# Layer 2's experts: picking the two largest of 16 gates by two rounds of a maximum instead of comparisons in pairs

## What is computed

```python
scores = jax.nn.softmax((xf @ gate_w.T).astype(jnp.float32), axis=-1)
orig = scores
scores = scores + gate_b
sg = scores.reshape(T, 4, 4)
group_scores = jax.lax.top_k(sg, 2)[0].sum(-1)
_, gidx = jax.lax.top_k(group_scores, 2)
keep = jax.nn.one_hot(gidx, 4).sum(axis=1) > 0
scores = jnp.where(keep[:, :, None], sg, -jnp.inf).reshape(T, 16)
_, idx = jax.lax.top_k(scores, 2)
weights = jnp.take_along_axis(orig, idx, axis=1)
...
h = jax.nn.silu(h1) * h3
yo = jnp.einsum('tei,eid->ted', h, We2) + be2
y = jnp.einsum('te,ted->td', combine, yo)
```

## Time and profile before

| | us |
|---|---|
| median of 3 runs (3043.07 to 3043.55) | 3043.09 |
| the profiled execution | 3035.05 |
| its span, first to last instruction | 3033.3 |
| PE busy in the span | 2791.1 (92%) |
| DVE busy | 2149.0 (71%) |
| ACT busy | 1706.9 (56%) |
| POOL busy | 1043.7 (34%) |

### The profile page before, as it was taken

How to read it: one execution, slowest core, us unless ns; L and a number is a source line. 1 busy time by engine, 2 the same in 40 slices (tenths; PEclk the granted TensorE clock), 3 DMA queues, 4 the chain that set the end, 5 groups by cost and what they waited for, 6 DMA issues and landing times.

```text
span 3033.3 us, 68982 instructions
## 1 busy us (share of the span) xinstructions
PE 2791.1 (92%) x25484; PEld 1876.1 (62%) x25484; DVE 2149.0 (71%) x5792; ACT 1706.9 (56%) x4109; POOL 1043.7 (34%) x1420
## 2 busy tenths in 40 slices
PE   6999999989999999999998799999989988998897
PEld 2666666666666666666666455577756655556675
DVE  6888888855666566666666688665667786887674
ACT  3877777873333377777776466634335443333565
POOL 7787778731000001111112345222333321004341
PEclk9999999999999999999999899999989999999999
DMA  3110111122000011111112544100054432334660
GB/s 104 30 29 17 29 29 30 29 72 99 15 1 1 10 25 30 30 30 30 30 30 65 150 140 131 45 1 15 1 150 136 121 92 57 84 72 130 195 173 26
DMA packets 194061, 188.15 MB, mean 62 GB/s; under 512 B 14416, under 2 KB 170256, under 8 KB 192960
## 3 DMA queue, kind: packets, MB, share of 16 engines
q1 hardware_dynamic: 193728, 183.73, 23.2%
HBM read 130.36 MB, written 53.31 MB: 61 GB/s over the span
## 4 chain that ended last, share of the span: by engine, by line
PE 64%; DVE 18%; ACT 6%; issue 5%; SPq 3%; DMA 2%; POOL 2%; DVEq 0%; ACTq 0%; POOLq 0%
PE pb L160 57%; ACT big L932 4%; PE pb L629 3%; SPq L1834 2%; DVE big L2153 2%; ACT big L157 2%; DVE big L802 2%; DVE big L231 1%; DVE big L785 1%; DMA big<-parts 1%; PE pb L562 1%; DVE big L713 1%; PE pb L2124 1%; DVE big L784 1%; DVE big L176 1%
## 5 line engine op out<-in xcount | busy, mean ns | idle before, releaser
L160 PE MATMUL pb<-big 64*128 64x256 bf16 (+13 forms) x20300 | 2525.4, 331 | 157.9 <-DVE big L2153 59.1
L160 PEld LDWEIGHTS pb<-big 128*128 128x128 f32 (+5 forms) x20300 | 1576.6, 145 | 904.9 <-issue 537.5
L157 ACT ACTIVATE big<-pb 128x512 f32<-128x512 f32 (+7 forms) x1444 | 825.9, 619 | 573.9 <-PE pb L160 333.8
L157 ACT ACTIVATE big<-pb,big 128x512 f32<-128x512 f32 (+2 forms) x536 | 315.9, 616 | 607.4 <-PE pb L160 511.7
L2153 DVE TENSOR_REDUCE big<-pb 128x4 f32<-128x1024 f32 (+1 forms) x256 | 278.1, 1086 | 111.5 <-PE pb L160 108.2
L171 POOL TENSOR_TENSOR big<-big 128x128 f32<-128x128 f32 x192 | 85.0, 457 | 684.2 <-DVE big L168 684.2
L932 ACT ACTIVATE big<-big 128x256 f32<-128x256 f32 x512 | 253.9, 497 | 70.9 <-DVE big L807 69.1
L932 ACT ACTIVATE big<-pb,big 128x128 f32<-128x128 f32 (+1 forms) x512 | 255.6, 513 | 64.5 <-DVE big L787 64.2
L802 DVE CUSTOM_DVE_ANT_0 big<-pb,big 128x256 f32<-128x256 f32 x512 | 186.6, 421 | 80.2 <-PE pb L160 79.9
L1011 POOL TENSOR_TENSOR big<-big 128x512 f32<-128x512 f32 x128 | 159.8, 1276 | 243.2 <-DMA big<-recip 243.2
L1508 DVE SCALAR_TENSOR_TENSOR big<-pb,big 128x128 f32<-128x128 f32 x512 | 144.0, 344 | 139.3 <-PE pb L160 138.5
(11 more groups left out here) (138 smaller groups left out, 2290.6 us busy)
## 6 DMA issues: line engine op xcount, KB each, us to landing
big<-parts SPq DMA_DIRECT2D x96, 512.0 KB, 4.1
parts<-big SPq DMA_DIRECT2D x384, 96.0 KB, 2.3
big<-recip SPq DMA_DIRECT2D x64, 512.0 KB, 6.5
big<-comb SPq DMA_DIRECT2D x32, 512.0 KB, 8.4
parts<-big SPq DMA_DIRECT2D x192, 64.0 KB, 2.1
big<-gates SPq DMA_DIRECT2D x8, 1024.0 KB, 6.2
big<-in_wf SPq DMA_DIRECT2D x1, 3072.0 KB, 14.9
big<-scratch SPq DMA_DIRECT2D x1, 3072.0 KB, 17.6
```

The costliest lines, as they stand in the source:

```text
L157: return e.activation(o, i, f, bias=bias, scale=scale)
L160: return e.matmul(o, l, r_, start=start, stop=stop, skip_group_check=True)
```

## The change

The pieces `top_a` and `top_b` keep their places, but no longer share the tiles between them. Each now handles all four tiles, and each finds one gate of every token: `take_largest` takes the maximum of the 16 gates, marks the places that equal it, multiplies the marks by 16, 15, ... 1, takes the maximum of that (the first place that has it), marks that place, and adds -3.0e38 to the gate there. `top_a` does this once, `top_b` a second time on what is left and then adds the two marks. All elementwise instructions have 64 columns, both maxima go from 64 columns to 4.

```diff
-        TRI = alloc(336)
-        TRI16, TRI8, TRI4 = TRI[:, 0:256], TRI[:, 256:320], TRI[:, 320:336]
+        TRI = alloc(96)
+        BACK16, TRI8, TRI4 = TRI[:, 0:16], TRI[:, 16:80], TRI[:, 80:96]
...
+        def take_largest(e, own, src, picked, tmp, largest):
+            back = BACK16.unsqueeze(1).to_broadcast([128, 4, 16])
+            every = largest.unsqueeze(2).to_broadcast([128, 4, 16])
+            e.tensor_reduce(largest, src, AXX, ALU.max).then_inc(own.sem, own.up())
+            e.wait_ge(own.sem, own.n)
+            e.tensor_tensor(tmp, src, every, ALU.is_equal).then_inc(own.sem, own.up())
+            e.wait_ge(own.sem, own.n)
+            e.tensor_tensor(tmp, tmp, back, ALU.mult).then_inc(own.sem, own.up())
+            e.wait_ge(own.sem, own.n)
+            e.tensor_reduce(largest, tmp, AXX, ALU.max).then_inc(own.sem, own.up())
+            e.wait_ge(own.sem, own.n)
+            e.tensor_tensor(picked, tmp, every, ALU.is_equal).then_inc(own.sem, own.up())
+            e.wait_ge(own.sem, own.n)
+            e.scalar_tensor_tensor(out=src, in0=picked, scalar=-3.0e38, in1=src, op0=ALU.mult, op1=ALU.add).then_inc(own.sem, own.up())
...
                 elif p == "top_a":
                     e.wait_ge(own.sem, own.n)
-                    keep_top2(e, own, glv[:, 0:2, :], 2, E, TRI16, gkv[:, 0:2, :], w1, w2)
+                    take_largest(e, own, glv, gkv, v3(w1), sm[:, 80:84])
                 elif p == "top_b":
-                    keep_top2(e, own, glv[:, 2:4, :], 2, E, TRI16, gkv[:, 2:4, :], w1, w2)
+                    e.wait_ge(own.sem, own.n)
+                    take_largest(e, own, glv, v3(w2), v3(w1), sm[:, 80:84])
+                    e.tensor_tensor(gkv, gkv, v3(w2), ALU.add).then_inc(own.sem, own.up())
+                    e.wait_ge(own.sem, own.n)
                     e.tensor_tensor(cm, gpv, gkv, ALU.mult).then_inc(combined, 1)
...
-    tri = [np.tril(np.ones((E, E)), -1).reshape(-1) for E in (16, 8, 4)]
-    c["tri"] = np.broadcast_to(np.concatenate(tri), (128, 336))
+    tri = [np.tril(np.ones((E, E)), -1).reshape(-1) for E in (8, 4)]
+    c["tri"] = np.broadcast_to(np.concatenate([16 - np.arange(16)] + tri), (128, 96))
```

## The result

| | before | after |
|---|---|---|
| median, us | 3043.08 (3035.17 to 3043.55) | 3004.6 (2998.88 to 3009.76) |
| profiled execution's span, us | 3033.3 | 2996.8 |
| chunk 2 of the expert steps, us (3.4 us of it at the lower clock before) | 31.24 | 26.53 |
| an ordinary chunk that no half-speed stretch touches, us | 29.62 | 26.53 |
| granted clock, mean over the span | 0.980 | 0.985 |

The account below looks back on a forecast made before the run. The chain that ended last lay on PE for 64% of the span and DVE for 18%, where alone a DVE edit pays. Terms 18.4 + 8.5 + 7.3 + 1 = 35.2 us off 3043.1 gave 3007.9 us, range 3003 to 3022.

Parts of the forecast that it names:

- The cost of the picking: DVE time of both pieces: 7.32 us a chunk falls to 1.42 and 1.82 us, 4.08 us less in each of eight chunks.
- The waits in the expert steps: Layer 2's expert steps: PE's waits for DVE go, 2.87 us in five chunks, 4.08 at the modulation, together 18.4 us.
- The spare: Expert steps, behind `top_b`: DVE would be early enough to end both PE waits with 1.2 us left over.
- The clock in the expert steps: Half-speed stretches of PE go with the waits, all but the one at the modulation: 8.5 us, bounds 0 and 10.5.
- The hosted steps: End of the attention before layer 2's expert steps: four PE waits shrink by 7.3 us, slower clock gives perhaps 1 us more.
- The rest: Smaller table and moved tiles: nothing taken; after step 54 all of the gain is handed on to layer 3 as a shift.
- The step that kept the 8.04 us between the median and the profiled execution: Whole kernel: the median stands 8.04 us above the profiled execution, and this was kept for the forecast time.
- Rival 1: Expert and hosted steps: waits go but the slow clock stays; gain 25.7 us, time 3017.4 us, chance 0.24.
- Rival 2: Picking on DVE: new instructions cost more than their nearest rows, so DVE saves 1.8 us a chunk; time 3029, chance 0.14.
- Rival 3: Picking on DVE: instruction count sets its time, so within 2 us of no change; time about 3043, chance 0.05.
- Rival 4: Picking on DVE stretched beside POOL's residual adds: 10.5 us a chunk against 7.32, 25 us longer, 3068; chance 0.05.

Follow-up runs that it names:

- steps_only: Changed kernel, but only chunks 2 to 7 pick by two maxima; hosted chunks 0 and 1 compare in pairs as before: 3010.7 us, ratio 0.9887.
- filler2: Changed kernel with two DVE memsets of 448 columns added behind each piece in chunks 2 to 7: 3010.7 us, ratio 0.9895 to the kernel before.
- filler1: Changed kernel with one DVE memset of 448 columns added behind each piece in chunks 2 to 7: 3007.7 us, ratio 0.9877 to the kernel before.
- filler3: Changed kernel with three DVE memsets of 448 columns added behind each piece in chunks 2 to 7: 3027.5 us, ratio 0.9947 to the kernel before.
- mod31: Changed kernel with the modulation for layer 3 moved three steps later, to step 31: 3007.5 us, ratio 0.9875 to the kernel before.
- hosted_only: Changed kernel, but only hosted chunks 0 and 1 pick by two maxima; chunks 2 to 7 compare in pairs as before: 3038.4 us, ratio 0.9983.
- old_places: Changed kernel with the table's old 336 columns kept, so tiles behind it stand where they stood before: 3008.2 us, ratio 0.9883 to the kernel before.
- filler4: Changed kernel with four DVE memsets of 448 columns added behind each piece in chunks 2 to 7: 3038.2 us, ratio 0.9981 to the kernel before.

## Why the prediction was right, point by point

**The cost of the picking.** Forecast 1.42 and 1.82 us, measured 1.43 and 1.82 us. The scalar_tensor_tensor that no row of before showed takes 0.23 us, as taken, and nothing waits for it. Taking the gap between dependent instructions from the `groups` chain carried this term. The Trainium skill, "VectorE: DVE Perf Modes", section "Rules for kernel authors", says to keep the number of chained instructions small. This trace doesn't bear that out as the only rule: one instruction more a chunk went with 4.08 us less, because 64 columns take 0.23 us and 512 take 0.68.

**The waits in the expert steps.** Forecast 5 x 2.87 + 4.08 = 18.4 us. An ordinary chunk went from 29.62 to 26.53 us, 3.09 us less and not 2.87, and it is 26.53 us long instead of the forecast 26.8. The chunk with the modulation went from 35.90 to 29.81 us, 6.1 us, of which 2.0 are clock, so 4.1 for the waits. Together 5 x 3.09 + 4.1 = 19.6 us. The small miss is in how I read the waits off the drawn ends: the lengths of the chunks are the better measure. The spare was put at 1.2 us and is 0.98.

**The clock in the expert steps.** Forecast 8.5 us, with one half-speed stretch left at the modulation. It went too: 23.9 us at the lower clock became none, which by the forecast's own counting is the upper bound of 10.5 us. The stage lost 29.7 us, so 29.7 - 19.6 = 10.1 us are left for the clock. That it came out near the upper bound is luck in part: the changed kernel's profile is its fastest execution, and with a wait at the modulation of the same length `steps_only` kept 3.4 us at half speed. By the measured stages the term was 1.6 us too small, and the waits 1.2 us.

**The hosted steps.** Forecast 1.69 + 1.91 + 2.17 + 1.55 = 7.3 us of waits and 1 us of clock. PE's waits of the changed kernel in the same three places that still have one, against the earlier trace rows:

```profile
2483.11 2.96 PE L160 MATMUL pb<-big 128*128 128x16 f32 x28 [0.99 <-DVE big L1901]
...
2506.38 3.58 PE L160 MATMUL pb<-big 64*128 64x256 bf16 x60 [1.86 <-DVE big L2173]
2510.68 1.90 PE L160 MATMUL pb<-big 64*128 64x256 bf16 x36 [0.72 <-DVE big L2173]
```

The first wait (1.69) is gone, the second and third are shorter by 1.91 and 2.17 us, as forecast. The fourth went from 1.55 to 0.72, 0.83 us and not 1.55. The reason is the clock in the run of matmuls ahead of it: before, 3.1 us of that run passed at half speed (it took 5.03 us), now none does (3.58 us), so PE comes to the wait 1.45 us sooner and finds more of it left. Where the run has a half-speed stretch and the picking is the new one, the wait is gone altogether, as forecast. In `filler2`, where the clock fell at 2506.8 us, one run goes through:

```profile
2507.38 6.70 PE L160 MATMUL pb<-big 64*128 64x256 bf16 x96 [1.86 <-DVE big L2181]
```

The same holds for `filler1`, `filler3`, `mod31` and `hosted_only`; at full clock `old_places` and `filler4` have 0.73 us left, as the changed kernel. The first wait behaves alike. Before, in the changed kernel, and in `old_places`, where the clock stayed at 1.00:

```profile
2469.39 3.38 PE L160 MATMUL pb<-big 64*128 64x256 bf16 x36 [3.41 <-DVE big L2153]
```

```profile
2474.41 3.23 PE L160 MATMUL pb<-big 64*128 64x256 bf16 x36 [3.41 <-DVE big L2173]
```

```profile
2474.19 1.90 PE L160 MATMUL pb<-big 64*128 64x256 bf16 x36 [3.40 <-DVE big L2173]
2477.07 0.63 PE L242 MATMUL pb<-big 128*128 128x128 f32 x4 [0.98 <-DVE big L2217]
```

So run and wait have to be taken together. From the start of the run to the start of the next one the first place went from 5.06 to 3.15 us and the fourth from 6.58 to 4.30. With the other two that is 1.91 + 1.91 + 2.17 + 2.28 = 8.3 us, and the stage lost 8.2. The forecast had the same 8.3 us as 7.3 of waits and 1 of clock: the sum is right, the two terms of it are not separate things. The spread of the clock is as large as the error: with the new picking the stage took 75.8 us (`old_places`, nothing at the lower clock) to 80.7 us (`mod31`, 17.1 us at it); with the old one 85.2 us, and 86.1 in `steps_only`, with 17.1 us. At equal time at the lower clock the gain is 5.4 us (86.1 - 80.7, both with 17.1) or 6.4 us (85.2 - 78.8 in `filler4`, both with 10.2), so part of the 8.2 us is how the half-speed stretches fell.

**The rest.** That the gain is handed on to layer 3 held: the stage behind the expert steps did not grow. The sum came out 35.2 us against 36.5 in the profiled spans, 36.8 by the ratio and 38.5 in the medians. The 5.0 us lost ahead of the change, 1.3 us of them with the moved tiles, and the 3.6 us gained behind it stand in no term of the forecast; that they take back half of what the two stages gave above it is luck. The step that kept the 8.04 us between the median and the profiled execution is the weakest one: the executions of the kernel before reach from 3035 to 3052 us, so a single profiled one can stand anywhere in that.

**The rivals.** Rival 1 (the clock stays slow) is refuted by the 1.00 over 218 us, and by 0 to 6.8 us at the lower clock in the expert steps of all six kernels with at most 2.07 us given back. Rival 2 (dearer instructions) by the DVE rows. Rival 3 (count) by the same rows and by `filler4`, whose ordinary chunk fits the line of DVE time. Rival 4 (POOL in the way): over all sixteen pieces no new instruction took more than 245 ns, so it didn't come up; in another place it might.

## What to carry to other kernels

When an engine off the bottleneck delays it only at one spot of a loop, measure the wait there and the work that an edit removes in front of it: at an unchanged clock the gain is the smaller of the two, the rest is spare, and a later edit of the same kind gains nothing there. Where the matmuls ahead of the wait ran at half speed, take run and wait together: at full speed the run shortens and part of the wait comes back, as in the fourth hosted place. Comparing in pairs costs n squared columns a row, a round of a maximum n, so at 16 gates the narrower instructions win though they are more; at 8 gates, in layer 1 of the kernel before, a whole picking for four tiles takes 1947.77 - 1945.51 = 2.26 us:

```profile
1942.88 0.19 DVE L1437 TENSOR_REDUCE big<-big 128x4 f32<-128x32 f32 x1
1943.10 0.19 DVE L1439 TENSOR_TENSOR big<-big 128x32 f32<-128x32 f32 x1
...
1945.51 0.42 DVE L1102 TENSOR_TENSOR big<-big 128x256 f32<-128x256 f32 x1
...
1947.77 0.19 DVE L1387 TENSOR_TENSOR big<-big 128x32 f32<-128x32 f32 x1
```

Two rounds would be thirteen instructions of 32 columns, eleven of them waited for, with 0.22 us from start to start (1943.10 - 1942.88). The eleven alone are 2.4 us, so there (an estimate, not run) it would lose. Count the half-speed stretches of the matmul engine that stand behind a wait as part of its price: here they added half as much again (10.1 us on 19.6).

## What the hardware showed that I had not expected

- Longer waits in the same place went with more falls of the clock. Five waits of 0.81 us (`filler2`) had no half-speed stretch behind them; five of 1.93 us (`filler3`) had three, and the stage 20.5 us more at the lower clock, which is 10 us of time. The number of waits was not varied by itself. The cost of DVE time is then uneven: the second pair of memsets cost 8.3 us in the expert steps, the third 16.8 us and the fourth 5.9 us, one execution each.
- Where tiles lie in SBUF changed the time of layer 0 by 1.3 us with the same instructions; profiles with the same table size agree there within 0.11 us.
- Executions of the same kernel differ more than the changes that one would like to measure: 3030 to 3050 us for `hosted_only`. Part of it is where the half-speed stretches fall, 86 to 147 us a profile in sum; the lengths of ordinary chunks agree within 0.02 us between profiles of kernels with the same picking.
